# Perceiver block, selective scan: terms spread by DMA, the drive on VectorE two steps ahead, GpSimd's weighing beside the next scan

## The reference

```python
h = einsum('bld,ed->ble', x, W_in); xb, zb = split(h, 2)        # 256 channels each
xb, zb = dwconv_silu(xb, Kx), dwconv_silu(zb, Kz)               # three taps, then SiLU
proj = einsum('blc,oc->blo', xb, W_xproj)                       # 32 + 8 + 8 rows
delta = clip(softplus(einsum('blr,cr->blc', dt_raw, W_dt) + b_dt), 1e-4, 1.0)
b_term, c_term = tanh(b_raw), tanh(c_raw)                       # 8 states each
a = softplus(A_log) + 1e-4
decay = clip(exp(-delta[..., None] * a), 1e-4, 1.0)
drive = (1.0 - decay) * (b_term[:, :, None, :] * xb[..., None])
# over the 512 tokens, for each of 256 channels and 8 states:
state = dec_t * state + drv_t
y = sum(state * c_t[:, None, :], axis=-1) + D * x_t
out = einsum('bld,ed->ble', concatenate([y, zb], -1), W_out)
```

## Time and profile before

| What | us |
|---|---|
| median of 3 runs | 3934.36 |
| lowest and highest | 3932.28, 3937.34 |
| the profiled execution's own time | 3938.72 |
| its span in the profile | 3937.4 |
| selective scan stage, first instruction to the next stage's first | 1734.7 to 1870.0 |
| granted clock of PE over the span, share of full speed | 0.95 |

### The profile page before, as it was taken

One profiled execution on the slowest core, in us unless ns is written; L12 is line 12 of the kernel. 1 busy time (PEld: TensorE's weight loads), 2 busy tenths in 40 slices (PEclk: granted clock), 3 DMA queues, 4 the chain that ended last, 5 costly groups with the idle time before them and its releaser, 6 DMA issues. The chain is left out here.

```text
span 3937.4 us, 46164 instructions
## 1 busy us (share of the span) xinstructions
PE 3641.8 (92%) x17900; PEld 2332.4 (59%) x17900; DVE 2545.2 (65%) x3446; ACT 1929.6 (49%) x1978; POOL 1820.2 (46%) x776
## 2 busy tenths in 40 slices
PE   6999899989999999977697999999999887799997
PEld 5777688755555555432575455555554366588886
DVE  2222234357777777637696877777776465699997
ACT  2112211145555555542584455555556321577785
POOL 1111111149999999824000499999998320100000
PEclk8999999999999999996798799999999998799999
DMA  6455655543333333100686333333331100799996
GB/s 252 162 190 189 194 176 175 186 134 87 87 89 78 84 86 86 37 23 0 264 351 237 83 86 86 87 80 84 86 86 38 49 1 24 282 367 378 375 376 254
DMA packets 215626, 589.61 MB, mean 150 GB/s; under 512 B 42577, under 2 KB 108145, under 8 KB 161777
## 3 DMA queue, kind: packets, MB, share of 16 engines
q1 hardware_dynamic: 176624, 513.24, 40.3%
q10 hardware_dynamic: 36864, 67.13, 4.6%
q0 software_dynamic: 1920, 6.29, 0.5%
HBM read 466.44 MB, written 120.06 MB: 149 GB/s over the span
## 5 line engine op out<-in xcount | busy, mean ns | idle before, releaser
L636 DVE TENSOR_REDUCE maxima<-psum 128x1 f32<-128x512 f32 x2048 | 1291.2, 684 | 388.1 <-PE psum L631 384.9
L745 ACT ACTIVATE pt<-psum 128x1024 f32<-128x1024 f32 x1024 | 1018.9, 1025 | 702.5 <-PE psum L656 696.8
L759 POOL TENSOR_TENSOR exp_sums<-pt 128x1024 f32<-128x1024 f32 x342 | 819.1, 2395 | 263.9 <-PE psum L672 130.7
L631 PE MATMUL psum<-ks,first_q 96*128 96x512 f32 x2048 | 814.6, 447 | 21.7 <-DMA first_q<-q_parts 10.5
L762 POOL TENSOR_TENSOR exp_sums<-exp_sums,pt 128x1024 f32<-128x1024 f32 x310 | 737.7, 2380 | 45.7 <-ACT pt L745 1.4
L668 PE MATMUL psum<-pt,vs 128*32 128x512 f32 x4096 | 675.8, 600 | 4.6 <-DVE head_rows L772 2.2
L631 PEld LDWEIGHTS psum<-ks,first_q 96*128 96x128 f32 x2048 | 393.7, 192 | 480.6 <-DVE maxima L636 323.9
L672 PE MATMUL psum<-exp_sums,constants 128*32 128x512 f32 x1408 | 671.6, 599 | 0.0
L656 PE MATMUL psum<-qs,ks 97*128 97x512 f32 x2048 | 648.5, 400 | 15.0 <-ACT pt L745 15.0
L1450 DVE TENSOR_TENSOR moe_cut<-moe_raw,moe_cut 128x2048 fp32r<-128x2048 f32 x244 | 557.3, 2291 | 57.0 <-ACT moe_cut L1392 52.0
L1392 ACT CAST moe_cut<-moe_raw 128x2048 fp32r<-128x2048 f32 x244 | 467.1, 1921 | 64.6 <-PE psum L97 64.6
(11 more groups left out here) (314 smaller groups left out, 4508.8 us busy)
## 6 DMA issues: line engine op xcount, KB each, us to landing
moe_raw<-in_moe_w SPq DMA_DIRECT2D x244, 1024.0 KB, 7.7
ks<-k_parts SPq DMA_DIRECT2D x384, 256.0 KB, 4.6
k_parts<-kparts ACTq DMA_DIRECT2D x256, 256.0 KB, 3.0
cx<-in_ctx SPq DMA_DIRECT2D x32, 1024.0 KB, 9.0
v_heads<-vrow SPq DMA_DIRECT2D x32, 1024.0 KB, 5.8
vs<-v_heads SPq DMA_DIRECT2D x32, 1024.0 KB, 5.3
first_q<-q_parts SPq DMA_DIRECT2D x96, 64.0 KB, 4.0
qs<-q_parts SPq DMA_DIRECT2D x96, 64.0 KB, 4.8
```

The lines of the kernel that those rows point to most:

```text
L631: pe.matmul(self.c.bank[self.FIRST_BANK + k % 3], self.first_q[s][:, t * P:(t + 1) * P], self.ks[s][part][0:3 * DH, at:at + CHUNK], start= ...
L636: dve.tensor_reduce(self.maxima[:, h % 2, i % TT, i // TT:i // TT + 1], self.c.bank[self.FIRST_BANK + k % 3], X, ALU.max).then_inc(*self.f ...
L745: act.activation(self.pt[:, self.slot(h, b) + i:self.slot(h, b) + i + 2, :], self.c.psum[:, at:at + 2, :], ACT.Exp).then_inc(*self.exp.up())
L759: engine.tensor_tensor(to, self.pt[:, slot:slot + R, :], self.pt[:, slot + R:slot + 2 * R, :], ALU.add).then_inc(*signal.up())
```

## The change

DMA takes over the spreading of b and c: SP stores both to a new scratch tensor in HBM, then loads each back onto 128 partitions, all 8 states at once (2 MB for b, 2 MB for c). PE's `spread_terms` and ACT's copies go. The Tanh for b is taken of -b_raw, so that `bc[0]` is -b. DVE makes the drive itself: after the clip, -b x `xb` into `drive`, then (`decay` - 1) x `drive` in one instruction; `rest` goes. These three instructions, `prepare(i + 2)`, stand behind the scan of step i. POOL keeps the weighing alone, and `weigh(i)` now waits for the last instruction of `prepare(i + 2)` as well. ACT only makes the decays.

```diff
+++ loads (SP)
+        for which in range(2):
+            sp.wait_ge(*self.bc_done.at(which + 1))
+            sp.dma_start(self.S["bc"][which], self.bc[:, which, :]).then_inc(*self.bc_out[which].up())
+        for which in range(2):
+            sp.wait_ge(*self.bc_out[which].at(1))
+            sp.dma_start(self.terms[:, which], self.S["bc"][which].rearrange("s n -> (s n)").partition_broadcast(P).rearrange("p (s n) -> p s n", s=DSTATE)).then_inc(*self.term_in[which].up())
+++ on_pe
         pe.wait_ge(*self.bc_done.at(2))
         pe.wait_ge(*self.w_out_in.at(1))
-        pe.wait_ge(*self.clipped.at(CB + 1))
-        def spread_terms(s):
-            ...
-        spread_terms(0)
-        spread_terms(1)
         pe.wait_ge(*self.silued.at(KD))
         for t in range(TT):
             output_part(t, range(CB, KD))
         for i in range(self.STEPS):
-            if i % CB == 0 and i // CB + 2 < DSTATE:
-                spread_terms(i // CB + 2)
             if i:
                 add(i - 1)
+++ on_act
         for which in range(2):
-            act.activation(self.bc[:, which, :], bank[5 + which][0:DSTATE, :], ACT.Tanh).then_inc(*self.bc_done.up())
+            act.activation(self.bc[:, which, :], bank[5 + which][0:DSTATE, :], ACT.Tanh, scale=(-1.0, 1.0)[which]).then_inc(*self.bc_done.up())
...
-        spread_terms(0)
         act.wait_ge(*self.clipped.at(CB + 1))
-        decays(0)
-        spread_terms(1)
         for i in range(self.STEPS):
-            if i + 1 < self.STEPS:
-                decays(i + 1)
-            if i % CB == 0 and i // CB + 2 < DSTATE:
-                spread_terms(i // CB + 2)
+            decays(i)
+++ on_dve
-        for i in range(self.STEPS):
+        def prepare(i):
             r = i % self.RING
             dve.wait_ge(*self.decayed.at(i + 1))
             dve.tensor_scalar(self.decay[:, r, :], self.decay[:, r, :], 1e-4, 1.0, ALU.max, ALU.min).then_inc(*self.step.up())
-            dve.wait_ge(*self.step.at(3 * i + 1))
-            dve.tensor_scalar(self.rest[:, r, :], self.decay[:, r, :], -1.0, 1.0, ALU.mult, ALU.add).then_inc(*self.step.up())
+            dve.tensor_tensor(self.drive[:, r, :], self.terms[:, 0, i // CB, :], self.conv[:, i % CB, :], ALU.mult).then_inc(*self.step.up())
             dve.wait_ge(*self.step.at(3 * i + 2))
-            dve.wait_ge(*self.driven.at(i + 1))
-            dve.tensor_tensor(self.drive[:, r, :], self.rest[:, r, :], self.drive[:, r, :], ALU.mult).then_inc(*self.step.up())
+            dve.scalar_tensor_tensor(self.drive[:, r, :], self.decay[:, r, :], 1.0, self.drive[:, r, :], ALU.subtract, ALU.mult).then_inc(*self.step.up())
+        dve.wait_ge(*self.silued.at(KD))
+        dve.wait_ge(*self.term_in[0].at(1))
+        prepare(0)
+        prepare(1)
+        for i in range(self.STEPS):
+            r = i % self.RING
             dve.wait_ge(*self.step.at(3 * i + 3))
             if i >= self.RING:
                 dve.wait_ge(*self.weighed.at(i - self.RING + 1))
             dve.tensor_tensor_scan(self.state[:, r, :], self.decay[:, r, :], self.drive[:, r, :], 0.0, ALU.mult, ALU.add).then_inc(*self.scanned.up())
+            if i + 2 < self.STEPS:
+                prepare(i + 2)
+++ on_pool
-        ...
+        pool.wait_ge(*self.term_in[1].at(1))
+        for i in range(self.STEPS):
             pool.wait_ge(*self.scanned.at(i + 1))
+            if i + 2 < self.STEPS:
+                pool.wait_ge(*self.step.at(3 * (i + 2) + 3))
             if i >= RING:
                 pool.wait_ge(*self.added.at(i - RING + 1))
             pool.tensor_tensor(self.part[:, i % RING, :], self.state[:, i % RING, :], self.terms[:, 1, i // CB, :], ALU.mult).then_inc(*self.weighed.up())
+++ perceiver
+            "bc": nc.dram_tensor("bc_rows", [2, DSTATE, TOK], F32, kind="Internal").ap(),
```

More of the change, by code:

```diff
@@ L811, with __init__ @@
     STEPS = DSTATE * CB
-    def __init__(self, c, A, x):
-        self.c, self.A, self.x = c, A, x
+    def __init__(self, c, A, S, x):
+        self.c, self.A, self.S, self.x = c, A, S, x
     def run(self):
@@ L833, in run @@
             self.decay = c.sb(st, "decay", [P, self.RING, TOK])
-            self.rest = c.sb(st, "one_minus_decay", [P, self.RING, TOK])
             self.drive = c.sb(st, "drive", [P, self.RING, TOK])
@@ L844, in run @@
             self.soft_in, self.soft_abs, self.soft_act, self.soft_out, self.clipped = c.signals(st, "soft_in soft_abs soft_act soft_out clipped")
-            self.spread_made, self.spread, self.decayed, self.driven = c.signals(st, "spread_made spread decayed driven")
+            self.decayed, = c.signals(st, "decayed")
+            self.bc_out, self.term_in = c.landings(st, "bc_out_0 bc_out_1"), c.landings(st, "term_in_0 term_in_1")
             self.step, self.scanned, self.weighed, self.added = c.signals(st, "scan_step scanned state_weighed state_added")
@@ L935, in on_act @@
         act.activation(self.soft_tmp[:], self.soft_tmp[:], ACT.Ln, bias=1.0).then_inc(*self.soft_act.up())
[L937 to L940, removed]
         def decays(i):
@@ L1004, in on_pool @@
         CB, RING = self.CB, self.RING
[L1005 to L1013, removed]
+        pool.wait_ge(*self.term_in[1].at(1))
+        for i in range(self.STEPS):
             pool.wait_ge(*self.scanned.at(i + 1))
-            pool.wait_ge(*self.spread.at(2 * (i // CB) + 2))
+            if i + 2 < self.STEPS:
+                pool.wait_ge(*self.step.at(3 * (i + 2) + 3))
             if i >= RING:
@@ L1018, in weigh @@
             pool.tensor_tensor(self.part[:, i % RING, :], self.state[:, i % RING, :], self.terms[:, 1, i // CB, :], ALU.mult).then_inc(*self.weighed.up())
[L1020 to L1026, removed]
 class Router:
@@ L1968, in perceiver @@
             attention.run()
-        SelectiveScan(c, A, x).run()
+        SelectiveScan(c, A, scratch, x).run()
         Experts(c, A, scratch, x, 0).run()
```

## The result

The changed kernel takes 3913.06 us (median of 6 runs, 3907.62 to 3915.83), the kernel before, beside it, 3935.73 us (median of 6). The ratio is 0.9941 (95% interval 0.9929 to 0.9952): 22.7 us less, where 19.5 had been forecast. The forecast time was 3915. Two executions further down (one of experiment 5, one of the kernel before beside experiments 8 and 9) ran in a slower state, at a mean granted clock of 0.73 and 0.64 in place of 0.95, and are left out of every median and ratio.

A forecast was written before the change was run, and what follows sets the result against it. DVE was taken as the bound, standing still while POOL works. Savings of 4.6 us at the start, 14.3 in the loop and 0.6 at the end make 19.5, so 3934.4 becomes 3915; range 3901 to 3924.

The forecast's parts named there:

- The bound: In the scan loop: DVE bounds it and stands still while POOL works, losing 0.94 + 0.95 = 1.9 us per step.
- The scan and POOL: In the loop: the scan and POOL's product block each other, assumed from the nearest rows; forecast case 60%.
- The first rival: In the loop: the scan lets POOL work, step about 3.15 us, 30.4 us saved, time 3904; chance 27%.
- The step: Scan to scan in the loop: 3.85 us with POOL; from scan 0 to scan 14, 14.3 us saved.
- The price: In each loop step: what POOL's product costs DVE, between 0.8 and 1.45 us, taken as 1.0.
- The unblocked part: In each loop step: DVE's scan to clip and three instructions without POOL, 1.14 + 1.69 = 2.83 us.
- The start: Start of the loop: the first scan starts at 1778.4 in place of 1782.98, 4.6 us earlier, 2.6 in the bad case.
- the doubt about 128 reads of one row: Start of the loop: only a small one-row load was on record; at 4 us a MB, b lands at 1777, not 1774.1.
- the rival of crawling loads: Start of the loop: loads from one row crawl; at 35 us for b the program ends at about 3942; slower, 5%.
- The end: From scan 14 to the end of the last weighing: 5.7 us in place of 6.3, 0.6 saved.
- The sum: Over the whole program: 4.6 + 14.3 + 0.6 = 19.5 us saved, with what follows the loop unchanged.
- the three pieces: In the scan stage: start of the loop 4.6 us, scan 0 to scan 14 14.3, end 0.6.

The follow-up runs named there:

- experiment 5: The changed kernel with the DMA part undone, so PE and ACT spread b and c again: 3922.37 us, ratio 0.9964 to the kernel before.
- experiment 8: The changed kernel with the drive in two PSUM banks and weigh(i) waiting for the second instruction of prepare(i + 2): 3896.63 us, ratio 0.9901 to the kernel before.
- experiment 9: The changed kernel itself measured once more, with nothing changed: 3916.36 us, ratio 0.9948 to the kernel before.
- experiment 4: The kernel before with only the DMA part added, b and c spread by DMA and the old loop kept: 3931.48 us, ratio 0.9986.
- experiment 1: The changed kernel with POOL weighing only 32 of 512 tokens per step, most of y left out: 3903.7 us in one run.
- experiment 2: The changed kernel with POOL's product replaced by a memset that reads nothing, the weighing left out: 3898.2 us in one run.
- Experiment 7: The changed kernel with the drive in two PSUM banks in place of SBUF: 3902.67 us, ratio 0.9921 to the kernel before.

## Why the prediction was right

**The bound.** That DVE bounds the loop, and by standing still beside POOL, is shown from both sides: with both holds the step is 4.65 us (experiment 4), with one 3.80, with none 2.78 to 2.79 (experiments 1, 2 and 8). One kernel shows it by itself, too: in the last two steps of the kernel before, POOL has no drive left to make, the L991 ahead of each of the last two scans is 0.69 us again, and a step is 3.70 us (scans at 1846.46, 1850.16 and 1853.87). So what a step gained is a hold: two of 0.94 and 0.95 us before, one of 1.02 after. Without its holds the old step is 4.65 - 1.89 = 2.76 us, as long as the new one (2.78): by this sum the new list of DVE, and its running two steps ahead, save nothing in the steady step. No run tests the running ahead by itself.

**The scan and POOL.** This was the assumption on which most hung, and it had no row. It holds, and experiments 1, 2 and 7 show it. The first rival, that the scan lets POOL work, is out; its argument, that the scan reads less per unit of time, has no bearing, because POOL's 32 columns waited for the whole scan. Experiment 7 shows what that rival would have looked like: a step of 3.02 us, for which it had 3.15. The rule of the Trainium skill that was cited ("SBUF — State Buffer", Who interferes with whom) states it as it was measured: the memset, which reads no SBUF, was let by, and with one input in PSUM the scan no longer contends.

**The step.** Forecast 3.85 us, measured 2.78 + 1.02 = 3.80. The forecast's own terms, 2.83 and 1.0, make 3.83; the loop was summed with 3.85. The price was taken between bounds of 0.8 and 1.45, and that it came within 0.02 is partly luck. The unblocked part was 0.05 too long: from start to start the scan has 1.14, the clip 0.32, the product 0.71 and the third instruction 0.61. All fourteen steps are 0.05 us shorter than forecast, which makes the loop's 0.7 us between 14.3 and 15.0.

**The start.** The loads were forecast to land 7.3 and, for c, some 12 us after issue; they took 6.9 and 11.4. So the doubt about 128 reads of one row is settled, and the rival of crawling loads is out. The stores took 1.5 us in place of 2.0. DVE began when the decay was there, as the forecast had it. Counted from the b and c rows, the first scan came where the kernel before would have it at 1778.0; the forecast was 1778.4. Saved 5.0 us against 4.6.

**The end.** 0.6 us, as forecast: the three weighings behind one another take 5.42 us.

**What was mis-sized.** The sum held that nothing moves outside these pieces. In the profile 2.4 us were lost ahead of the b and c rows and 3.0 won behind the last weighing; this nearly cancels. Both follow PE's granted clock. In the kernel before the stretch of the output product (1859.4 to 1870.0) had 0.77, in the changed one (1835.5 to 1843.7) it had 1.00, and the product L891 took 7.13 us in place of 9.51. Busy time by engine and granted clock over the two stretches, before and after:

```profile
1859.40:1870.00 10.60, 9.51 (x16) 3.90 (x16) 2.77 (x4) 0.00 (x1) 0.00 (x0) 0.77 0.00 0
1835.50:1843.70 8.20, 7.13 (x16) 2.96 (x16) 2.76 (x4) 0.00 (x0) 0.00 (x0) 1.00 0.00 0
```

Ahead of the rows it was the other way: the first block of `h` was copied 16.2 us after the stage's start in place of 13.8. The first is not due to the change (experiment 9). Whether the shorter tail is, stays open. From the last weighing to the stage's end it was 13.5 us before and 13.9 in experiment 4, which have the old loop, and 10.5, 11.6 and 10.7 in the two profiles of the changed kernel and in experiment 5, which have the new one; but the variants with the new DVE list have 11.1 to 13.5 us. Its length goes roughly with the granted clock over it: 0.99 at 10.5 us, 0.87 at 11.6 and 12.9, 0.69 at 13.9. So the three pieces that were forecast at 19.5 us gave 20.6; that the other two nearly cancel, so that the whole stage gave 21.2, is luck.

**The difference of the medians,** 22.7 us, is 1.5 more than the stage's 21.2. The second measurement gave 3935.25 - 3916.36 = 18.9. The two lie on both sides of it, and nothing on record points at a further cause.

## What to carry to other kernels

Before work is moved to GpSimd, price the hold and not only the work: a 128x512 float32 product that would take VectorE 0.60 us cost it 1.02 us as a delay when GpSimd did it beside a scan with two SBUF inputs. In this kernel, with one input of those instructions in PSUM, the same product ran beside them at no cost; then it paid to choose its moment so that it ended before the next clip (3.02 us a step became 2.78). When a forecast hangs on one pair of engines that the trace does not show side by side, look for rows of the same kind of operands (here: two SBUF inputs), not of the same operation. And look at every instruction that the product can reach: the clip, with one SBUF input, was held as well.

## What the runs showed of the hardware that was not expected

GpSimd's product of 32 columns waited as long for the scan as one of 512 did: the wait depends on the other's instruction, not on one's own size (1.05 us, of which 0.25 us would be needed). A scan with its second input in PSUM takes 1.21 us, no longer than with both in SBUF (1.22). And 4 MB spread over 128 partitions from two rows of 16 KB landed 11.8 us after the first issue (1763.59 to 1775.4), no slower than the four loads of different data in the earlier trace rows (12.35 us from the first issue to the last landing).
